# One kernel, five edits: the order of row sends, two accumulators for most experts, and the last sums on two engines

## The chip, the cores and the metric

The kernel runs on one core of a Trainium2 chip. The time is the device time of one execution in microseconds. Three runs of the kernel before gave 907.73, 908.15 and 908.41 us, median 908.15 us.

## The reference

The layer takes x of 8 batches, 512 rows, 256 features. The first half is attention in a window, the second half a mixture of 64 experts:

```
h = layernorm(x) * (1 + ca) + sa;   x = x + ga * attention(h)      # 16 heads, |q - k| <= 64
h = layernorm(x) * (1 + cb) + sb;   x = x + gb * experts(h)
# experts: sigmoid scores, 4 of 8 groups, 8 of 64 experts per row, weights * 2.5;
# at most 256 rows per expert; y = (silu(h Wg) * (h Wu)) Wd; every row adds up its 8 scaled y
```

All is float32 from outside; some products of the attention are in bf16 pieces.

## The kernel before, in words

There is no planner: every engine has its instruction stream written out in order, and semaphores tie the streams together. The work has two stages.

**Attention and routing.** Eight batches go through a loop (`body`) of 20 slots each: four groups of four heads (g), five key tiles (u), slot = 5g + u. A slot makes two tiles of scores, two exponentials on ScalarE (`exps`, L886, semaphore `exp`, two counts a slot), and VectorE takes maxima. The value products (`values`, L1159, semaphore `pv`, two counts a tile) are not made in their own slot: PE makes those of tiles 0, 1 and 2 of a group in slot u = 3, and those of tiles 3 and 4 in slot u = 0 of the next group (L1248 to L1250). Beside this, tables say in which slot the next batch is projected and the batch behind is normalised and routed. One step of these tables is `c_rstd` (L719): four small GpSimd operations that turn a half batch's variance (`mv2`, from VectorE, L1498) into the scale and shift that ScalarE then uses in `c_xhat` (L918). ScalarE works in order, so its exponentials stand behind `c_xhat`, and PE's scores wait for exponentials.

When a batch is routed, each of its rows goes to its 8 slots in DRAM (`slots_d`). That is 32 indirect DMAs a batch, issued by GpSimd (`send`, L731, and `send_some`, L751), up to two in a slot. The first of a slot waits until all exponentials of the slots before are done (count 2*slot). The second waits until all value products of the slots before are done (`pv`, count 2*slot, L757). GpSimd is in order too, so `c_rstd` of a later slot stands behind both. What is left of the last batches is sent after the loop: 8 sends of the last batch but one, `c_rstd(last, 0)`, 2 sends, `c_rstd(last, 1)`, 18 sends, and the 32 sends of the last batch (L807 to L820).

**Experts.** For each of the 64 experts SP loads 256 rows (`load_slots`, L634, a ring of 12), PE turns them, multiplies (L1394), and multiplies again (L1404); ScalarE scales the result into one of six buffers (`scale_y`, L1012), and GpSimd adds the rows into an accumulator in DRAM by two indirect DMAs (`scatter`, L822). There are three accumulators, `acc_d`. Expert e uses number `ACC[e]`, which is e % 3 up to expert 53 and e % 2 from there (L438). A scatter waits until the scatter before it into the same accumulator has landed (L842). Accumulator 0 starts as x. SP also loads weights, for experts 36 and up when the buffer of the expert 36 before is free (L650 to L652).

**The end.** SP loads accumulator 2 into `f2` (`load_f2`, L628, 32 DMAs of 128 KB) and the gates into `fg` (1 MB), waits for the last scatters, and loads accumulators 0 and 1 batch by batch into `fa` (L660, 16 DMAs of 512 KB). For each batch VectorE makes three operations of 128x1024 float32 (L1861, L1863, L1865): add the halves of `fa`, add `f2`, multiply by `fg`. SP stores each batch when its three are done (L665), in the order of the batches, all on the queue of the loads.

Of the kernel before, what the change touches and what calls it, by code (L numbers as in the profile page):

```python
# [25 lines left out]
ALU = mybir.AluOpType  # L26
# [19 lines left out]
HW = D + E + 4  # L46
# [18 lines left out]
    exp=10 * QUADS, pv=10 * QUADS, oTs=QUADS, oTp=QUADS, rec=QUADS, on=QUADS,  # L65
# [164 lines left out]
def build(nc, x, w_qkv, b_qkv, w_out, b_out, gate_w, gate_bias, w_gate, w_up, w_down, c, wmod, out):  # L230
    with ExitStack() as ctx:
        sems = {name: ctx.enter_context(nc.semaphore("s_" + name)) for name in PER}

        def sem(name):
            return ctx.enter_context(nc.semaphore(name))
# [20 lines left out]
        def after(eng, name, bt, k, apart=False):  # L256

            v = bt.b * PER[name] + k
            if isinstance(v, int) and v <= 0:
                return  # L260
            if apart or eng is nc.sync or eng is nc.gpsimd:
                hold(eng, sems[name], v)
            else:
                eng.wait_ge(sems[name], v)
# [31 lines left out]
        s_fg = sem("gate_rows_loaded")  # L296
# [18 lines left out]
        mod_d = dram("mod_d", [B, 5, D])  # L315
        slots_d = dram("slots_d", [SLOTROWS, HW])
        acc_d = [dram(f"acc_d{i}", [ACCROWS, D]) for i in range(3)]

        att = ExitStack()
        sb = lambda name, shape, dt=F32: sbt(att, name, shape, dt)  # L320
# [82 lines left out]
        sb = lambda name, shape, dt=F32: sbt(moe, name, shape, dt)  # L403
        NW, NX, NY = 36, 12, 6
# [3 lines left out]
        for i in range(NW):  # L408
# [8 lines left out]
        end = ExitStack()  # L417
        sb = lambda name, shape, dt=F32: sbt(end, name, shape, dt)
        fg = sb("fg", [P, B, D])
        sb("beyond_the_start", [P, 7656 - B * D])  # L420
        NF = 8
        f2 = [sb(f"f2_{i}", [P, T, D]) for i in range(B)]
        fa = [sb(f"fa{i}", [P, 2, T, D]) for i in range(NF)]
        end.close()
        eng_moe = dict(
            w_ld=[sem(f"weights_loaded{i}") for i in range(NW)],
# [3 lines left out]
            sg=sem("silu_done"),  # L430
            hm=sem("hidden_done"), yp=sem("expert_out_made"), yc=sem("expert_out_scaled"),
            f2_ld=sem("third_sums_loaded"),
            f_ld=[sem(f"sums_loaded{i}") for i in range(NF)], fsum=sem("last_sums"),
            f_st=sem("out_stored"),
        )
        mo = eng_moe

        ACC = [e % 3 if e < 54 else e % 2 for e in range(E)]  # L438
        NCONST = 26
        NSET = 4  # L440
        BLANKS = 32
# [33 lines left out]
        def rows_added(eng, e):  # L475

            eng.wait_ge(mo["y_st"][e % NY], 32 * (e // NY + 1))
# [21 lines left out]
        def _(sp):  # L499
# [125 lines left out]
            load_c(last)  # L625
            rows = slots_d.rearrange("(h p e) c -> p h e c", h=2, p=P)

            def load_f2(b):  # L628
                rows_added(sp, max(e for e in range(E) if ACC[e] == 2) + b)
                for t in range(T):  # L630
                    sp.dma_start(f2[b][:, t, :], acc_d[2][b * S:(b + 1) * S, :].rearrange("(p t) d -> p t d", p=P)[:, t, :]
                                 ).then_inc(mo["f2_ld"], 16)

            def load_slots(e):  # L634
                if e >= NX:
# [11 lines left out]
            for e in range(E):  # L647
                if NX <= e + 8 < E:
                    load_slots(e + 8)
                if e + NW < E:  # L650
                    sp.wait_ge(mo["yp"], e + 1)
                    load_w(slice(e + NW, e + NW + 1), e)  # L652

            for b in range(B):
                load_f2(b)
            sp.dma_start(fg[:], mod_d[:, 4, :].unsqueeze(0).to_broadcast([P, B, D])).then_inc(s_fg, 16)
            for e in range(E - NY, E):
                rows_added(sp, e)

            def load_f(i, n):  # L660
                for k in range(2):
                    sp.dma_start(fa[n][:, k], acc_d[k][0:N, :].rearrange("(b p t) d -> b p t d", b=B, p=P)[i]
                                 .rearrange("o p t d -> p (o t) d")).then_inc(mo["f_ld"][n], 16)

            def store_f(i, n):  # L665
                sp.dma_start(out[i].rearrange("o (p t) d -> p (o t) d", p=P), fa[n][:, 0]).then_inc(mo["f_st"], 16)

            for b in range(B):
                if b >= NF:
                    sp.wait_ge(mo["f_st"], 16 * (b - NF + 1))  # L670
                load_f(slice(b, b + 1), b % NF)
                if b >= NF - 1:
                    sp.wait_ge(mo["fsum"], 3 * (b - NF + 2))
                    store_f(slice(b - NF + 1, b - NF + 2), (b + 1) % NF)
            for b in range(B - NF + 1, B):
                sp.wait_ge(mo["fsum"], 3 * (b + 1))
                store_f(slice(b, b + 1), b % NF)
            sp.wait_ge(mo["f_st"], 16 * B)


# [1 line left out]
        def _(pool):  # L682
            gp = nc.gpsimd
            n = [0]
# [66 lines left out]
            def send_some(bt, rows, now, slot):  # L751

                for n, i in enumerate(rows):
                    if n == 0:
                        after(pool, "exp", now, 2 * slot)
                    else:
                        after(pool, "pv", now, 2 * slot)  # L757
                    send(bt, i)

            def body(prev, now, nxt):  # L760
# [61 lines left out]
            def scatter(e):  # L822
                begins = ACC[e] > 0 and ACC.index(ACC[e]) == e
                for h in range(2):
                    pool.wait_ge(mo["yc"], 2 * e + h + 1)
                    if begins:
                        pool.indirect_dma_start(
                            out=acc_d[ACC[e]][:, :], in_=ys[e % NY][:, h, :], in_offset=None,
                            out_offset=bass.IndirectOffsetOnAxis(ap=xg[e % NX][:, h, IDCOL:IDCOL + 1].bitcast(U32), axis=0),
                            bounds_check=last_acc, oob_is_err=True).then_inc(mo["y_st"][e % NY], 16)  # L830
                        continue
                    pool.indirect_dma_start(  # L832
                        out=acc_d[ACC[e]][:, :], in_=ys[e % NY][:, h, :], in_offset=None,
                        out_offset=bass.IndirectOffsetOnAxis(ap=xg[e % NX][:, h, IDCOL:IDCOL + 1].bitcast(U32), axis=0),
                        bounds_check=last_acc, oob_is_err=True, compute_op=ALU.add).then_inc(mo["y_st"][e % NY], 16)
# [3 lines left out]
            for e in range(E):  # L839
                same = [f for f in range(e) if ACC[f] == ACC[e]]  # L840
                if same:
                    rows_added(pool, same[-1])  # L842
                scatter(e)


        @block.scalar
        def _(act):
# [174 lines left out]
            for e in range(E):  # L1022
                silu(e)
                if e < E - 1:
                    take_x(e + 1)
                if e > 0:
                    scale_y(e - 1)
            scale_y(E - 1)

# [390 lines left out]
        def _(dve):  # L1420
# [434 lines left out]

            dve.wait_ge(s_fg, 16)
            dve.wait_ge(mo["f2_ld"], 16 * B * T)
            for b in range(B):
                a = fa[b % NF]
                dve.wait_ge(mo["f_ld"][b % NF], 32 * (b // NF + 1))  # L1860
                v.tensor_tensor(a[:, 0], a[:, 0], a[:, 1], ALU.add).then_inc(mo["fsum"], 1)  # L1861
                dve.wait_ge(mo["fsum"], 3 * b + 1)
                v.tensor_tensor(a[:, 0], a[:, 0], f2[b][:], ALU.add).then_inc(mo["fsum"], 1)  # L1863
                dve.wait_ge(mo["fsum"], 3 * b + 2)
                v.tensor_tensor(a[:, 0], a[:, 0], fg[:, b, :].unsqueeze(1).to_broadcast([P, T, D]), ALU.mult  # L1865
                                ).then_inc(mo["fsum"], 1)


_INS = ["L0_attn_x", "L0_attn_w_qkv", "L0_attn_b_qkv", "L0_attn_w_out", "L0_attn_b_out", "L0_ffn_gate_w",
# [18 lines left out]
```

## Time and profile before

| what | us |
|---|---|
| median of three runs | 908.15 |
| the profiled execution | 907.57 |
| its span, first to last instruction | 905.8 |
| PE busy | 681.8 (75%) |
| VectorE busy | 478.9 (53%) |
| ScalarE busy | 394.4 (44%) |
| GpSimd busy | 509.8 (56%) |

The span is what the rows below are measured in, from 0 to 905.8; 1.8 us of the profiled execution lie around it. An engine can be far from fully busy over the span and still set the end in one stage, so the stages are read one by one: attention from about 20 to 525, the rest of the routing to 613, experts from 613 to 868, the last sums from 868 to the end.

### The profile page before, as it was taken

The numbers are of one execution on the slowest core, as the hardware profiler recorded it, in microseconds if no ns is written. First come the engines' busy times: TensorE is split into PE (matmuls) and PEld (weight loads), VectorE is DVE, ScalarE is ACT, GpSimd is POOL, SyncE is SP. The second block draws the span as 40 slices with busy tenths as digits, with TensorE's granted clock in tenths as the row PEclk, the third lists the DMA queues.
The fourth block names the chain that finished last, engine by engine and source line by source line (L and its number), as shares of the span: only waits on it lengthen the run. The fifth ranks groups of instructions, "written<-read, shape, count | busy, mean of one in ns | idle before, by whom it ended". The sixth has DMA issues, their size and how long they took to land.

```text
span 905.8 us, 15461 instructions
## 1 busy us (share of the span) xinstructions
PE 681.8 (75%) x4760; PEld 466.9 (52%) x4787; DVE 478.9 (53%) x1964; ACT 394.4 (44%) x876; POOL 509.8 (56%) x519
## 2 busy tenths in 40 slices
PE   5679899999999999999797942006999888888000
PEld 3335556556566565565455522005888777676000
DVE  3065559869698697786787736201222222222048
ACT  2336566657566566665644511002444333334000
POOL 4000002057577476575767767772788888888810
PEclk9869999999999999999989975557999999999555
DMA  8684896748757577373536794107999998898997
GB/s 325 164 339 164 276 354 211 245 139 271 266 172 259 175 257 254 117 237 123 191 120 182 210 292 120 28 4 224 274 288 266 266 175 160 162 159 160 204 307 318
DMA packets 168334, 191.47 MB, mean 211 GB/s; under 512 B 22137, under 2 KB 150677, under 8 KB 168252
## 3 DMA queue, kind: packets, MB, share of 16 engines
q1 hardware_dynamic: 132220, 134.15, 46.6%
q0 software_dynamic: 30336, 38.03, 20.1%
q10 hardware_dynamic: 5696, 18.30, 5.3%
q8 instruction: 39, 0.64, 0.3%
q14 instruction: 43, 0.35, 0.1%
HBM read 100.64 MB, written 110.67 MB: 233 GB/s over the span
## 4 chain that ended last, share of the span: by engine, by line
PE 47%; POOL 14%; DMA 11%; DVE 10%; issue 9%; ACT 6%; ACTq 1%; SPq 1%; POOLq 0%; DVEq 0%
POOL acc_d L832 8%; PE outT L1171 7%; DMA acc_d<-ys,xg 7%; POOL slots_d L746 5%; PE scoresT L1394 5%; PE scoresT L1151 4%; PE stageA L1092 4%; PE scores L1129 4%; PE scoresT L1155 4%; PE stageA L1110 3%; PE stageC L1212 3%; ACT PT L890 2%; DMA Qs<-MT 2%; DVE junk L1453 2%; PE turns L1181 2%
## 5 line engine op out<-in xcount | busy, mean ns | idle before, releaser
L746 POOL DMA_INDIRECT slots_d<-H,dest x256 | 260.8, 1019 | 155.2 <-issue 87.9
L832 POOL DMA_INDIRECT acc_d<-ys,xg x124 | 191.6, 1545 | 55.0 <-issue 29.2
L1453 DVE CUSTOM_DVE_ANT_0 junk<-scores,mask 128x256 bf16<-128x256 f32 (+1 forms) x512 | 170.9, 387 | 72.1 <-PE scores L1129 70.8
L890 ACT ACTIVATE PT<-scoresT 128x512 f32<-128x512 f32 (+1 forms) x320 | 150.5, 509 | 47.5 <-PE scoresT L1155 45.6
L1394 PE MATMUL scoresT<-xgT,wgu 128*128 128x256 f32 x512 | 125.5, 388 | 17.5 <-ACT xgT L1005 17.4
L1151 PE MATMUL scoresT<-mask,identb 128*128 128x512 bf16 (+1 forms) x320 | 110.3, 345 | 18.7 <-ACT PT L890 14.5
L1394 PEld LDWEIGHTS scoresT<-xgT,wgu 128*128 128x128 f32 x512 | 95.4, 192 | 40.8 <-ACT xgT L1005 27.9
L1155 PE MATMUL scoresT<-Qs,Ks 98*128 98x256 bf16 (+1 forms) x640 | 110.9, 255 | 0.0
L1129 PE MATMUL scores<-Ks,Qs 96*128 96x256 bf16 (+1 forms) x512 | 93.7, 266 | 4.0 <-DVE mrowmax L1453 1.8
L1155 PEld LDWEIGHTS scoresT<-Qs,Ks 98*128 98x128 bf16 x640 | 64.0, 100 | 38.2 <-issue 8.6
L1171 PE MATMUL outT<-PT,Va 128*32 128x256 f32 (+1 forms) x1280 | 80.4, 356 | 1.8
L1842 DVE COPY xgT<-stageA 128x256 f32<-128x256 f32 x32 | 13.6, 425 | 118.2 <-PE stageA L1382 118.2
L874 ACT ACTIVATE parts<-stageA,bqk 128x512 bf16<-128x512 f32 x78 | 53.6, 687 | 42.3 <-PE stageA L1092 37.3
L1382 PE MATMUL scores<-ident,xg 128*128 128x128 f32 x128 | 24.9, 277 | 47.2 <-DMA xg<-slots_d 47.2
L1842 DVE COPY xgT<-stageC 128x256 f32<-128x256 f32 x32 | 13.6, 425 | 75.6 <-PE stageC L1382 75.6
L1151 PEld LDWEIGHTS scoresT<-mask,identb 128*128 128x128 bf16 x320 | 31.8, 99 | 39.8 <-ACT PT L890 22.2
L1005 ACT ACTIVATE xgT<-scores 128x256 f32<-128x256 f32 x64 | 24.7, 386 | 62.5 <-PE scores L1382 62.5
L1129 PEld LDWEIGHTS scores<-Ks,Qs 96*128 96x128 bf16 x512 | 44.4, 99 | 13.1 <-DVE mrowmax L1453 7.0
L1092 PE MATMUL stageA<-hT,wqkv 128*128 128x512 f32 x104 | 50.2, 605 | 0.0
L1171 PEld LDWEIGHTS outT<-PT,Va 128*32 128x32 f32 (+1 forms) x1280 | 28.9, 109 | 40.9 <-issue 25.2
L1018 ACT ACTIVATE ys<-outT,xg 128x256 f32<-128x256 f32 x64 | 26.9, 471 | 52.4 <-DMA acc_d<-ys,xg 45.3
L1018 ACT ACTIVATE ys<-turns,xg 128x256 f32<-128x256 f32 x64 | 26.9, 471 | 50.8 <-DMA acc_d<-ys,xg 43.1
(260 smaller groups left out, 1059.9 us busy)
## 6 DMA issues: line engine op xcount, KB each, us to landing
xg<-slots_d SPq DMA_DIRECT2D x64, 324.0 KB, 4.0
slots_d<-blank ACTq DMA_DIRECT2D x26, 648.0 KB, 5.2
parts_d<-parts SPq DMA_DIRECT2D x32, 384.0 KB, 3.4
Qs<-parts_d SPq DMA_DIRECT2D x96, 128.0 KB
Ks<-parts_d SPq DMA_DIRECT2D x90, 128.0 KB
acc_d<-zero SPq DMA_DIRECT2D x32, 272.0 KB
wgu<-L_ffn_w_gate_dram SPq DMA_DIRECT2D x64, 128.0 KB, 3.6
wgu<-L_ffn_w_up_dram SPq DMA_DIRECT2D x64, 128.0 KB, 3.7
```

What stands on the lines that cost most here:

```text
L746: pool.indirect_dma_start(out=slots_d[:, :], in_=H2[bt.par][:, t, :], in_offset=None, out_offset=bass.IndirectOffsetOnAxis(ap=dest[bt.par] ...
L832: pool.indirect_dma_start(out=acc_d[ACC[e]][:, :], in_=ys[e % NY][:, h, :], in_offset=None, out_offset=bass.IndirectOffsetOnAxis(ap=xg[e % ...
L874: sc_.activation(parts[:, j, k, :], bank[:, :], ACT.Identity, scale=SCALE if f < 2 else 1.0, bias=bqk[:, f:f + 1]).then_inc(sems["part"], 1)
L890: sc_.activation(PT[m % NPT][:, :, 0:w], src, ACT.Exp).then_inc(sems["exp"], 1)
L1018: sc_.activation(ys[e % NY][:, h, :], yb[:, h * D:(h + 1) * D], ACT.Copy, scale=xg[e % NX][:, h, D + e:D + e + 1]).then_inc(mo["yc"], 1)
L1092: last = mm(bank[:, :], wqkv[:, k, f * P:(f + 1) * P], hT[:, k, BAND:BAND + S], start=(k == 0), stop=(k == C - 1))
L1129: last = mm(bS[n % 2][:, i * 2 * P + lo:i * 2 * P + hi], q[0:MROW, h, t * P:(t + 1) * P], kk[0:MROW, h, t * P + lo:t * P + hi], start=True ...
L1151: mm(bST[m % 2][:, 0:2 * (hi - lo)].rearrange("p (h q) -> p h q", h=2), identb[:], half.unsqueeze(1).to_broadcast([P, 2, hi - lo]), start= ...
L1155: last = mm(bST[m % 2][:, i * (hi - lo):(i + 1) * (hi - lo)], kk[0:KROWS, h, u * P:(u + 1) * P], q[0:KROWS, h, lo:hi], start=False, stop=T ...
L1171: last = mm(bO[32 * j:32 * j + 32, lo:hi], Va[bt.par][rows, tile_of(u), HQ * g + j, :], PT[m % NPT][rows, i, 0:hi - lo], start=(u == 0), s ...
L1394: last = mm(bST[par][:, a * CAP:(a + 1) * CAP], wgu[e % NW][:, a, k, :], xgT[par][:, k, :], start=(k == 0), stop=(k == C - 1))
L1453: ins = v.tensor_tensor_reduce(out=junk[:, i, lo:hi], in0=bS[n % 2][:, i * 2 * P + lo:i * 2 * P + hi], in1=mask[:, lo:hi], scale=1.0, scal ...
```

## The change

- **Sends.** The second send of a slot waits for count 2*slot + 1 of `exp`, the slot's first exponential, and no longer for value products.
- **Accumulators.** `ACC[e]` is e % 3 up to expert 26 and e % 2 from there.
- **Third sums.** The 32 loads of `f2` are issued in the loop over experts, one in each of the iterations 27 to 58, each behind the expert's products, and the load of `fg` in iteration 59. They stood behind the loop. Four of the eight `f2` buffers lie in memory below the experts' own, the others behind it.
- **Last sums.** Batches 1 and 4 are summed by GpSimd, by the same three operations; VectorE sums the other six. The stores stay in the order of the batches, and all 16 loads of `fa` are issued ahead of the first store.
- **First output.** ScalarE scales the output of expert 0 in iteration 0, ahead of `silu(1)`; it stood in iteration 1.

```diff
-        ACC = [e % 3 if e < 54 else e % 2 for e in range(E)]
+        THIRD_ENDS = 27
+        POOL_SUMS = (1, 4)
+        ACC = [e % 3 if e < THIRD_ENDS else e % 2 for e in range(E)]
...
-            def load_f2(b):
-                rows_added(sp, max(e for e in range(E) if ACC[e] == 2) + b)
-                for t in range(T):
-                    sp.dma_start(f2[b][:, t, :], acc_d[2][b * S:(b + 1) * S, :].rearrange("(p t) d -> p t d", p=P)[:, t, :]
-                                 ).then_inc(mo["f2_ld"], 16)
+            def load_f2(b, t):
+                rows_added(sp, max(e for e in range(E) if ACC[e] == 2))
+                sp.dma_start(f2[b][:, t, :], acc_d[2][b * S:(b + 1) * S, :].rearrange("(p t) d -> p t d", p=P)[:, t, :]
+                             ).then_inc(mo["f2_ld"], 16)
...
-            for b in range(B):
-                load_f2(b)
-            sp.dma_start(fg[:], mod_d[:, 4, :].unsqueeze(0).to_broadcast([P, B, D])).then_inc(s_fg, 16)
+                if THIRD_ENDS <= e < THIRD_ENDS + B * T:
+                    sp.wait_ge(mo["yp"], e + 1)
+                    load_f2(*divmod(e - THIRD_ENDS, T))
+                if e == THIRD_ENDS + B * T:
+                    sp.wait_ge(mo["yp"], e + 1)
+                    sp.dma_start(fg[:], mod_d[:, 4, :].unsqueeze(0).to_broadcast([P, B, D])).then_inc(s_fg, 16)
...
-                    if n == 0:
-                        after(pool, "exp", now, 2 * slot)
-                    else:
-                        after(pool, "pv", now, 2 * slot)
+                    after(pool, "exp", now, 2 * slot + min(n, 1))
...
+            for n, b in enumerate(POOL_SUMS):
+                pool.wait_ge(mo["f_ld"][b], 32)
+                a = fa[b]
+                gp.tensor_tensor(a[:, 0], a[:, 0], a[:, 1], ALU.add).then_inc(mo["psum"], 1)
+                pool.wait_ge(mo["psum"], 3 * n + 1)
+                gp.tensor_tensor(a[:, 0], a[:, 0], f2[b][:], ALU.add).then_inc(mo["psum"], 1)
+                pool.wait_ge(mo["psum"], 3 * n + 2)
+                gp.tensor_tensor(a[:, 0], a[:, 0], fg[:, b, :].unsqueeze(1).to_broadcast([P, T, D]), ALU.mult
+                                 ).then_inc(mo["psum"], 1)
...
-                if e > 0:
+                if e == 0:
+                    scale_y(0)
+                if e > 1:
                     scale_y(e - 1)
```

## Rows read from the trace of the kernel before

**Rows 1.** The page's chain that ended last, shares by line.

```profile
POOL acc_d L832 8%; PE outT L1171 7%; DMA acc_d<-ys,xg 7%; POOL slots_d L746 5%; PE scoresT L1394 5%; PE scoresT L1151 4%; PE stageA L1092 4%; PE scores L1129 4%; PE scoresT L1155 4%; PE stageA L1110 3%; PE stageC L1212 3%; ACT PT L890 2%; DMA Qs<-MT 2%; DVE junk L1453 2%; PE turns L1181 2%
```

**Rows 2.** Windows: stretch, its us; busy of PE, PEld, DVE, ACT, POOL; clock; DMA; GB/s.

```profile
197.00:256.00 59.00, 55.61 (x467) 35.52 (x470) 47.35 (x221) 37.37 (x79) 38.78 (x46) 1.00 0.68 227
...
495.00:500.00 5.00, 4.21 (x30) 2.13 (x32) 3.36 (x11) 3.03 (x7) 3.25 (x4) 0.57 0.48 139
```

**Rows 3.** Timeline, slots 4 to 6 of the last batch: start, duration, instruction, idle before.

```profile
487.75 0.30 DVE L1498 BATCH_NORM_AGGREGATE mv<-stats 128x2 f32<-128x6 f32 x2
490.73 0.45 POOL L723 TENSOR_SCALAR ve<-mv 128x2 f32<-128x2 f32 x1
491.80 0.30 DVE L1498 BATCH_NORM_AGGREGATE mv<-stats 128x2 f32<-128x6 f32 x2
492.69 1.09 ACT L918 ACTIVATE H<-x,nmean,rs 128x256 f32<-128x256 f32 x2 [4.61 <-POOL nmean L729]
494.32 0.39 PE L1151 MATMUL scoresT<-mask,identb 128*128 128x512 bf16 x1 [3.03 <-ACT PT L890]
```

**Rows 4.** Timeline of GpSimd: first send of the last batch but one, and `c_rstd(last, 0)`.

```profile
525.70 0.97 POOL L746 DMA_INDIRECT slots_d<-H,dest  x1 [6.16 <-DVE H L1710]
...
541.13 0.22 POOL L723 TENSOR_SCALAR ve<-mv 128x2 f32<-128x2 f32 x1
```

**Rows 5.** Timeline of GpSimd: scatters of experts 3, 60, 62 and the last.

```profile
637.80 1.55 POOL L832 DMA_INDIRECT acc_d<-ys,xg  x1 [1.08 <-ACT ys L1018]
...
848.88 1.54 POOL L832 DMA_INDIRECT acc_d<-ys,xg  x1 [0.57 <-DMA acc_d<-ys,xg]
...
857.02 1.54 POOL L832 DMA_INDIRECT acc_d<-ys,xg  x1 [1.04 <-DMA acc_d<-ys,xg]
...
862.56 1.54 POOL L832 DMA_INDIRECT acc_d<-ys,xg  x1 [0.30 <-issue]
```

**Rows 6.** The last sums: timeline, the window 872 to 896, and the stores' issues.

```profile
868.36 8.87 SPq L662 DMA_DIRECT2D fa<-acc_d  x16
873.41 1.23 DVE L1861 TENSOR_TENSOR fa<-fa 128x1024 f32<-128x1024 f32 x1 [35.16 <-DMA fa<-acc_d]
901.50 1.22 DVE L1865 TENSOR_TENSOR fa<-fa,fg 128x1024 f32<-128x1024 f32 x1
872.00:896.00 24.00, 0.00 (x0) 0.00 (x0) 22.18 (x19) 0.00 (x0) 0.00 (x0) 0.50 1.02 410
L666 SPq DMA_DIRECT2D out_dram<-fa x8: 332/332/1058, 877.3 to 902.8; - x8
```

**Rows 7.** Scatters, issue to landing: stretch 690 to 726, then 726 to 827; timeline beside expert 58.

```profile
DMA to landing us min/median/max: 4.8/5.5/6.3
DMA to landing us min/median/max: 3.7/4.0/5.3
840.91 0.84 ACT L1018 ACTIVATE ys<-outT,xg 128x256 f32<-128x256 f32 x2 [3.11 <-DMA acc_d<-ys,xg]
```

**Rows 8.** Timeline: GpSimd and VectorE side by side, three places.

```profile
149.66 1.22 DVE L1514 TENSOR_TENSOR x<-x,mr 128x1024 f32<-128x1024 f32 x1
148.74 1.04 POOL L708 TENSOR_TENSOR rs<-ve,half_c 128x4 f32<-128x4 f32 x1
149.86 1.11 POOL L710 TENSOR_SCALAR nmean<-mv 128x4 f32<-128x4 f32 x1
142.99 0.24 POOL L727 TENSOR_SCALAR nmean<-mv 128x2 f32<-128x2 f32 x1
13.68 0.90 POOL L795 MEMSET Va<- 128x960 f32 x1
14.20 0.41 DVE L1439 COPY mcol<-modT 128x4 f32<-128x4 f32 x1
```

**Rows 9.** Timeline of GpSimd: a shorter memset and a copy.

```profile
12.80 0.55 POOL L791 MEMSET zero<- 128x544 f32 x1
111.00 0.29 POOL L717 COPY hT<-hT 128x128 f32<-128x128 f32 x1 [21.47 <-ACT hT L863]
```

More of the change, by code:

```diff
@@ L419, in build @@
         fg = sb("fg", [P, B, D])
-        sb("beyond_the_start", [P, 7656 - B * D])
+        f2 = [sb(f"f2_{i}", [P, T, D]) for i in range(B // 2)]
+        sb("beyond_the_start", [P, 7656 - B * D - B // 2 * T * D])
         NF = 8
-        f2 = [sb(f"f2_{i}", [P, T, D]) for i in range(B)]
         fa = [sb(f"fa{i}", [P, 2, T, D]) for i in range(NF)]
+        sb("beside_experts", [P, NW * 3 * D - NF * 2 * T * D + NX * 2 * HW + 2 * C * CAP + 4 * CAP + NY * 2 * D])
+        f2 += [sb(f"f2_{i}", [P, T, D]) for i in range(B // 2, B)]
         end.close()
@@ L432, in build @@
             f2_ld=sem("third_sums_loaded"),
-            f_ld=[sem(f"sums_loaded{i}") for i in range(NF)], fsum=sem("last_sums"),
+            f_ld=[sem(f"sums_loaded{i}") for i in range(NF)], fsum=sem("last_sums"), psum=sem("last_sums_by_gpsimd"),
             f_st=sem("out_stored"),
@@ L668, in _ @@
             for b in range(B):
[L669 to L677, printed above, removed]
+                load_f(slice(b, b + 1), b)
+            for b in range(B):
+                sp.wait_ge(mo["psum" if b in POOL_SUMS else "fsum"], 3 * sum((i in POOL_SUMS) == (b in POOL_SUMS) for i in range(b + 1)))
+                store_f(slice(b, b + 1), b)
             sp.wait_ge(mo["f_st"], 16 * B)
@@ L843, in _ @@
                 scatter(e)
+            pool.wait_ge(s_fg, 16)
+            pool.wait_ge(mo["f2_ld"], 16 * B * T)
+            for n, b in enumerate(POOL_SUMS):
[7 more added lines that the diff above has]
+                                 ).then_inc(mo["psum"], 1)
         @block.scalar
@@ L1857, in _ @@
             dve.wait_ge(mo["f2_ld"], 16 * B * T)
+            n = 0
             for b in range(B):
-                a = fa[b % NF]
-                dve.wait_ge(mo["f_ld"][b % NF], 32 * (b // NF + 1))
+                if b in POOL_SUMS:
+                    continue
+                dve.wait_ge(mo["f_ld"][b], 32)
+                a = fa[b]
                 v.tensor_tensor(a[:, 0], a[:, 0], a[:, 1], ALU.add).then_inc(mo["fsum"], 1)
-                dve.wait_ge(mo["fsum"], 3 * b + 1)
+                dve.wait_ge(mo["fsum"], n + 1)
                 v.tensor_tensor(a[:, 0], a[:, 0], f2[b][:], ALU.add).then_inc(mo["fsum"], 1)
-                dve.wait_ge(mo["fsum"], 3 * b + 2)
+                dve.wait_ge(mo["fsum"], n + 2)
                 v.tensor_tensor(a[:, 0], a[:, 0], fg[:, b, :].unsqueeze(1).to_broadcast([P, T, D]), ALU.mult
                                 ).then_inc(mo["fsum"], 1)
+                n += 3
 _INS = ["L0_attn_x", "L0_attn_w_qkv", "L0_attn_b_qkv", "L0_attn_w_out", "L0_attn_b_out", "L0_ffn_gate_w",
```

## The prediction

> **What bounds the kernel now.** I read the chain of waits first. No line holds more than 8% of it, and GpSimd's scatters and sends and their DMAs are high in it [rows 1]. So each stage has its own limit, and I went stage by stage.
>
> In the attention the windows show PE busy 55.6 of 59 us with GpSimd at 38.8 [rows 2]: PE paces it. One place is different. In the last batch VectorE has the first half's statistics at 488.05, but GpSimd begins `c_rstd` only at 490.73. ScalarE stands idle 4.61 us for it with its exponentials behind, and PE loses 3.03 us [rows 3]. The granted clock then reads 0.57 in 495 to 500 [rows 2], the lower level for most of that stretch. After the attention GpSimd sends without a pause: from 525.70, released by VectorE's routing, 12 sends stand ahead of `c_rstd(last, 0)` at 541.13 [rows 4]. What is gained before 525 therefore carries through to the experts.
>
> In the experts GpSimd is the bound. From expert 3 (637.80) to the last (862.56) are 121 steps between scatters. At 1.848 us each that is 223.6 of the 224.8 us between, and the two excesses of [rows 5] over the usual 0.30 idle (0.27 at 848.88, 0.74 at 857.02) are 1.0 of the rest. PE needs 3.03 us an expert (its products of the timeline stand so far apart from 627 to 694), GpSimd 3.70.
>
> In the last sums, `fa` loads are issued from 868.36 and the first batch is there at 873.4. VectorE's 24 operations run to 902.72, nearly back to back, 3.66 us a batch; the last store is issued at 902.8 and the shortest store takes 2.6 us. The DMA engines move 410 GB/s from 872 to 896 [rows 6]. VectorE is the bound, the DMAs close behind.
>
> **Sends.** The exponential of a slot is done long before the value products of the slots ahead. I put the send table, the ends of the 320 exponentials and the value products into a queue of 1.28 us per send. With the old wait it gives 490.67 for the late `c_rstd` (the trace: 490.73), with the new one GpSimd is free at 486.3. So it starts at 488.1, when the statistics are there, 2.6 us earlier. The next thing is then late: the second half's statistics end at 492.1 [rows 3], its `c_rstd` takes 1.65 us, and the next exponentials stand behind that half on ScalarE, from 494.9 and not 495.6. I take -0.6 us. Bounds: 0 if VectorE's four products behind it bind, and -3.7 if the 3 us stall and with it the lower clock go (2.5 to 3 us of PE's work between 496 and 502 ran at about half speed). In the other batches the queue shows `c_rstd` released by VectorE with either wait, so nothing there; no instruction is added.
>
> **First output.** ScalarE's scaling of expert 0 moves about 2.2 us forward into idle time. GpSimd waits for expert 3 (idle 1.08 at 637.80 [rows 5]), which this does not move. Cost and gain are 0; below and above by at most that 0.78 of excess.
>
> **Accumulators and third sums.** With two accumulators a scatter waits for the expert two before it. Its second scatter starts 3 x 1.85 = 5.55 us ahead, less 0.3 us of dispatch: no bubble if it lands within 5.25 us. The 840.91 row is expert 56 landing, 5.23 us after its start at 835.68; expert 58 then started on time. From 726 to 827 the landings by the profile's own count are 3.7 to 5.3 us, median 4.0; with weights loading beside them, 690 to 726, median 5.5 [rows 7]. ScalarE's waits (scale of e waits for e - 6) give the full delay of the slower scatter of experts 27 to 57: mean 4.7, four of 31 over 5.24, excess 0.3 us in sum. The `f2` loads put 128 KB beside each expert, a third of the weights' 384 KB. With landings 0.1 us later the excess is about 0.7 us: +0.7. Bounds: +0.3 with no delay, and +5.8 if they cost a third of the weights' 1.5 us (34 experts x 0.17).
>
> On SP the first `f2` load waits until expert 26 has landed (729.9), and `load_slots(36)` stands behind it. PE wants those rows at about 733.6 and gets them at 734.3; ScalarE then waits anyway until 737.0. Nothing is lost, and with that cover gone it is 1.7 us.
>
> In return the burst at the end goes. Both present bubbles lie under `f2` and `fg` loads: -1.0. The last scatter was issued at 862.56 and `fa` loads could start 5.8 us later; without a 1 MB load beside it I take the mean of 4.7 above and 0.2 for SP's start: -0.9.
>
> **Last sums.** VectorE loses 6 of 24 operations: 6 x 1.22 = 7.3 us. GpSimd gets six operations of 128x1024 with two inputs, of which the trace has none. A memset (no input) costs 0.90 for 960 and 0.55 for 544 elements: 0.84 ns an element and 0.10 fixed. The copy of 128 elements, 0.29 us, is 1.48 ns an element, so one input adds 0.65 [rows 8, 9]. Two inputs: 2.13 ns x 1024 + 0.10 = 2.3 us. Ends: 0.96 (the memset alone) and 3.2 (the copy's whole 0.29 per 128, plus a pass). I take 2.3, the copy being nearest.
>
> Can they run beside VectorE? A GpSimd operation of four elements that needs about 0.24 us took 1.11 us under a 1.22 us VectorE operation of just this kind (128x1024, both inputs in SBUF) and ended 0.09 us behind it. In the other direction a VectorE copy of four columns begun during the 0.90 us memset ended with it [rows 8]. So one waits for the other. VectorE and GpSimd then share 18 x 1.22 + 6 x 2.3 = 35.8 us, where VectorE alone took 29.3. Loads arrive one batch per 1.05 MB / 0.41 = 2.6 us and are ahead of this. The end moves by 13.8 - 7.3 = +6.5 us; by the ends of the price -1.5 and +11.9.
>
> The Trainium skill, "SBUF — State Buffer", section "Who interferes with whom", says that a VectorE instruction with two SBUF inputs contends with a GpSimd one that reads SBUF, and that the first to issue holds the shared pair for its whole instruction. The first part agrees with the 1.11 us; "whole" does not quite: the GpSimd operation of 148.74 to 149.78 reached 0.12 us into the VectorE one, which still took 1.22 [rows 8]. By "whole" the sum stays +6.5, by a hold of the reading alone it falls by some 0.1 us an operation, to +5.9. The Trainium skill, "GPSIMD Engine Reference", section "3.1 Elementwise — side-by-side cycle accounting", gives 4497 ns for 2048 elements; half of that is 2.25 us, which would make the term +6.2; no row here shows such an operation.
>
> **Sum.** +6.5 - 1.0 - 0.9 + 0.7 - 0.6 = +4.7 us on the span, 905.8 to 910.5. The profiled execution was 907.57, 0.6 under the median, so on the median: 912.9 us.
>
> **Rivals.**
> 1. *The engines run side by side* (faster). Then VectorE is done with its six batches at about 896.2, held up by loads, and the DMAs bind: 12.6 MB in all, of which 1.05 are in at 873.4, and 11.5 / 0.41 = 28.1 us more, 901.5 against 902.8 + 2.6 = 905.4 now: -3.9. With the other -1.8 this is 902.4 us. For: GpSimd is idle there. Against: the 1.11 us. It decides when six GpSimd operations cost VectorE less than 7.3 us together.
> 2. *Serial but cheaper, or the clock kept.* At 1.6 us an operation the term is +2.3, and with up to 3 us more in the last batch's attention the total lies at -2 to +2.5: 908.7. For: sizes are extrapolated eightfold. Against: the copy's slope.
> 3. *GpSimd shut out until VectorE pauses.* It then finishes batch 4 last, at the same 909, and the stores of 4 to 7 go out after it: 2.1 MB / 0.41 = 5.1 us where one took 2.6. 915.4.
> 4. *Two accumulators stall the scatters.* +5.8 for +0.7: 918.0. For: 5.5 us medians under loads. Against: 4.0 without.
>
> **Chances.** Forecast 0.50 (own range 910.5 to 914.5), rival 1 0.20, rival 2 0.20, rivals 3 and 4 0.05 each. 0.2% is 1.8 us, about what a measurement here can tell from no change. Faster by more: rival 1 and 0.08 of rival 2, 0.28. Within: 0.10 from rival 2. Slower by more: the forecast, rivals 3 and 4 and the rest of rival 2, 0.62. The range must reach rival 1's centre below and the forecast's worst above: 901 to 916.
>
> **What would show it.** Six GpSimd operations of 128x1024 of about 2.3 us or more, VectorE's 18 lengthened or with gaps of 2 us between them, and its last one ending near 907.4 (right); VectorE still 1.22 us beside them (rival 1). Idle before L723 near 490 with VectorE as releaser, and PE's stall moved to about 495. Scatters with idle over 0.30 released by a DMA between experts 27 and 63, some 0.7 us in sum. No `f2` load after 845. Wrong would be a GpSimd operation overlapping full-speed VectorE ones, or an excess over 3 us in the scatters.

## The result, and the profile after

| what | before | after |
|---|---|---|
| median of 12 runs, us | 907.87 (904.51 to 909.94) | 914.76 (911.01 to 923.15) |
| the profiled execution | 907.57 | 913.71 |
| its span | 905.8 | 911.9 |
| PE busy | 681.8 | 682.2 |
| VectorE busy | 478.9 | 481.9 |
| GpSimd busy | 509.8 | 527.6 |

The change makes the kernel slower: ratio 1.0089, 95% interval 1.0065 to 1.0112. That is 8.1 us (5.9 to 10.2); the two medians lie 6.9 us apart. The forecast was 912.9 us in a range of 901 to 916. GpSimd's extra 17.8 us come of its six sums. VectorE lost six operations and is still 3.0 us busier, which is the first sign of what happened.

Cut at the instants on which the prediction rests, the two profiled executions compare like this:

| stretch | before | after | difference |
|---|---|---|---|
| start to expert 3's scatter | 637.80 | 635.58 | -2.2 |
| expert 3's scatter to the last one | 224.76 | 229.69 | +4.9 |
| last scatter to VectorE's first sum | 10.85 | 8.93 | -1.9 |
| VectorE's first to last sum | 29.31 | 34.60 | +5.3 |
| from there to the end | 3.1 | 3.1 | 0 |

The sum is +6.1, which is 911.9 less 905.8. The chain of waits on the profile's page of the kernel after, shares by line, shows the growth in the scatters more roughly: the scatters, at 8% in [rows 1], are at 10%.

```profile
POOL acc_d L829 10%; PE outT L1182 7%; POOL slots_d L746 5%; PE scoresT L1405 5%; PE stageA L1103 5%; PE scoresT L1162 4%; DMA acc_d<-ys,xg 4%; PE scores L1140 4%; PE scoresT L1166 4%; PE stageA L1121 3%; PE stageC L1223 3%; ACT PT L899 2%; DVE junk L1464 2%; DMA Qs<-MT 2%; PE turns L1192 2%
```

**Last sums.** VectorE's timeline after, from its first sum (start, duration, instruction, idle before). In [rows 6] each of the 24 took 1.22 or 1.23.

```profile
874.20 1.23 DVE L1875 TENSOR_TENSOR fa<-fa 128x1024 f32<-128x1024 f32 x1 [32.82 <-DMA fa<-acc_d]
...
880.22 1.22 DVE L1875 TENSOR_TENSOR fa<-fa 128x1024 f32<-128x1024 f32 x1 [2.27 <-DMA fa<-acc_d]
881.47 3.25 DVE L1877 TENSOR_TENSOR fa<-fa,f 128x1024 f32<-128x1024 f32 x1
884.75 3.25 DVE L1879 TENSOR_TENSOR fa<-fa,fg 128x1024 f32<-128x1024 f32 x1
...
897.76 1.21 DVE L1875 TENSOR_TENSOR fa<-fa 128x1024 f32<-128x1024 f32 x1
...
907.57 1.23 DVE L1879 TENSOR_TENSOR fa<-fa,fg 128x1024 f32<-128x1024 f32 x1
```

And GpSimd's timeline after, for the same stretch:

```profile
877.80 2.34 POOL L847 TENSOR_TENSOR fa<-fa 128x1024 f32<-128x1024 f32 x1 [10.98 <-DMA fa<-acc_d]
880.22 3.42 POOL L849 TENSOR_TENSOR fa<-fa,f 128x1024 f32<-128x1024 f32 x1
883.72 3.20 POOL L851 TENSOR_TENSOR fa<-fa,fg 128x1024 f32<-128x1024 f32 x1
```

Read the two lists side by side. GpSimd's first sum runs while VectorE waits for loads and takes 2.34 us. Its other five each take 3.20 to 3.42 us and lie beside a VectorE sum that is lengthened as well. Five VectorE sums of 3.25 to 3.36, from 881.47 to 897.76, are five pairs. When GpSimd is done, VectorE is back at 1.21 at once.

**Scatters.** GpSimd's timeline after at four places that answer to [rows 5]: experts 3, 27, 56 and the last.

```profile
635.58 1.55 POOL L829 DMA_INDIRECT acc_d<-ys,xg  x1 [1.26 <-ACT ys L1027]
...
725.20 1.55 POOL L829 DMA_INDIRECT acc_d<-ys,xg  x1 [0.86 <-DMA acc_d<-ys,xg]
...
837.44 1.55 POOL L829 DMA_INDIRECT acc_d<-ys,xg  x1 [1.71 <-DMA acc_d<-ys,xg]
...
865.27 1.55 POOL L829 DMA_INDIRECT acc_d<-ys,xg  x1 [0.30 <-issue]
```

GpSimd's waits from 620 to 870 (waited for: us in total, times, longest), with the least, median and most from issue to landing of a scatter in 728 to 827 (4.0 in the middle in [rows 7]):

```profile
POOL acc_d L829 <- DMA acc_d<-ys,xg: 8.9, 12, 1.7
DMA to landing us min/median/max: 3.1/4.4/6.8
```

The idle before a scatter over the usual 0.30, released by a DMA, is called a bubble below. After expert 3 they add up to 5.2 us in ten places, where before they were 1.0 in two.

SP's timeline after, for the first row of [rows 6]: the loads of `fa` begin 3.92 us behind the last scatter, where it was 5.80.

```profile
869.19 9.30 SPq L667 DMA_DIRECT2D fa<-acc_d  x16
```

**Sends.** GpSimd's timeline after, for [rows 3] and [rows 4]: `c_rstd` of the last batch's halves, and the first send of the last batch but one.

```profile
488.08 0.23 POOL L723 TENSOR_SCALAR ve<-mv 128x2 f32<-128x2 f32 x1
...
491.93 0.22 POOL L723 TENSOR_SCALAR ve<-mv 128x2 f32<-128x2 f32 x1 [2.23 <-DVE mv L1509]
...
523.59 0.97 POOL L746 DMA_INDIRECT slots_d<-H,dest  x1 [6.35 <-DVE H L1721]
```

The first `c_rstd` starts at 488.08 and not 490.73; the second now waits for VectorE and no longer for sends. The windows after (us; busy of PE, PEld, DVE, ACT, POOL; clock; DMA; GB/s), of which the first answers to the second of [rows 2]; and the last one to that of [rows 6]:

```profile
495.00:500.00 5.00, 4.71 (x39) 2.55 (x40) 2.86 (x11) 1.95 (x5) 3.99 (x4) 0.67 0.43 124
500.00:505.00 5.00, 4.79 (x51) 3.17 (x50) 4.26 (x18) 3.33 (x8) 3.77 (x5) 0.99 0.56 160
872.00:896.00 24.00, 0.00 (x0) 0.00 (x0) 19.32 (x9) 0.00 (x0) 17.89 (x6) 0.50 0.99 393
```

The windows of the kernel before for the second of these stretches:

```profile
500.00:505.00 5.00, 4.86 (x40) 2.86 (x36) 2.04 (x11) 2.02 (x5) 3.78 (x5) 0.74 0.54 159
```

The granted clock is back at its upper level (2.4 GHz) almost from 500 on, and not only within 500 to 505. What that is worth can be read from ScalarE's exponentials. The timeline of the kernel before, the first one behind the second half's `c_xhat` and the one three slots later, in which 8.1 us pass:

```profile
495.63 1.07 ACT L890 ACTIVATE PT<-scoresT 128x512 f32<-128x512 f32 x2
...
503.76 0.38 ACT L890 ACTIVATE PT<-scoresT 128x256 f32<-128x256 f32 x1 [0.19 <-PE scoresT L1155]
```

And of the kernel after, in which 7.0 us pass:

```profile
494.66 1.06 ACT L899 ACTIVATE PT<-scoresT 128x512 f32<-128x512 f32 x2
...
501.62 0.91 ACT L899 ACTIVATE PT<-scoresT 128x256 f32<-128x256 f32 x2 [0.29 <-PE scoresT L1166]
```

### The profile page after: what moved, and what is told of

Same layout as the page of the kernel before. It is cut to its first block, busy times and chain, and to the rows that moved or that the text cites. A ratio compares the mean times of both kernels' runs of the same rounds, so it can differ in the third digit from the quotient of the medians.

```text
span 911.9 us, 15494 instructions
## 1 busy us (share of the span) xinstructions
PE 682.2 (75%) x4760; PEld 468.1 (51%) x4787; DVE 481.9 (53%) x1958; ACT 395.7 (43%) x876; POOL 527.6 (58%) x525
## 4 chain that ended last, share of the span: by engine, by line
PE 46%; POOL 16%; DVE 11%; issue 11%; DMA 9%; ACT 5%; SPq 1%; ACTq 1%; POOLq 0%; DVEq 0%
POOL acc_d L829 10%; PE outT L1182 7%; POOL slots_d L746 5%; PE scoresT L1405 5%; PE stageA L1103 5%; PE scoresT L1162 4%; DMA acc_d<-ys,xg 4%; PE scores L1140 4%; PE scoresT L1166 4%; PE stageA L1121 3%; PE stageC L1223 3%; ACT PT L899 2%; DVE junk L1464 2%; DMA Qs<-MT 2%; PE turns L1192 2%
## 5 line engine op out<-in xcount | busy, mean ns | idle before, releaser
L1162 PEld LDWEIGHTS scoresT<-mask,identb 128*128 128x128 bf16 x320 | 31.7, 99 | 37.8 <-ACT PT L899 18.7
L1393 PEld LDWEIGHTS scores<-ident,xg 128*128 128x128 f32 x128 | 18.3, 144 | 54.4 <-DMA xg<-slots_d 47.9
```

Source lines behind the costliest of these rows:

```text
L1162: mm(bST[m % 2][:, 0:2 * (hi - lo)].rearrange("p (h q) -> p h q", h=2), identb[:], half.unsqueeze(1).to_broadcast([P, 2, hi - lo]), start= ...
L1393: last = nc.tensor.transpose(bank[:, h * P:(h + 1) * P], xg[e % NX][:, h, k * P:(k + 1) * P], ident[:])
```

## The experiments

Every kernel but three was executed 6 to 12 times, beside the kernel before on the same chip; `x7_memsets`, `x9_first_output` and `x10_one_batch` were executed once, so only their profiles are read. The ratio is an estimate with its 95% interval and needn't equal the quotient of the two medians. Apart from the last sums, which are steady, executions differ by some 2 us (the last batch's attention starts at 470.6 to 474.0 in these profiles), so the profiles are compared by stretch. `x2`, `x3`, `x5`, `x6` and `x10` have the `f2` buffers where the changed kernel has them.

| kernel | us, beside before | ratio, 95% | bubbles | last scatter to first `fa` load | VectorE's sums |
|---|---|---|---|---|---|
| before | | | 1.01 | 5.80 | 29.31 |
| after | 914.76, 907.87 | 1.0089 (1.0065 to 1.0112) | 5.23 | 3.92 | 34.60 |
| x1_sends | 905.77, 906.48 | 0.999 (0.9968 to 1.0013) | 1.50 | 6.45 | 29.31 |
| x2_two_accumulators | 909.93, 906.48 | 1.0045 (1.0026 to 1.0064) | 7.30 | 3.88 | 29.32 |
| x3_two_engines | 913.14, 906.48 | 1.009 (1.0066 to 1.0114) | 0.47 | 6.94 | 34.89 |
| x4_all_but_two_engines | 906.79, 906.48 | 1.0015 (0.9993 to 1.0037) | 4.74 | 3.86 | 29.32 |
| x5_two_accumulators_late_loads | 905.55, 907.07 | 0.9981 (0.9963 to 0.9999) | 2.73 | 6.56 | 29.32 |
| x6_three_accumulators_other_loads | 906.56, 907.07 | 0.9993 (0.9975 to 1.001) | 2.73 | 3.94 | 29.32 |
| x7_memsets | 904.56, 907.07 | | 6.55 | 3.81 | 23.83 |
| x8_sends_gates_early | 903.16, 907.07 | 0.9957 (0.9934 to 0.998) | 0.90 | 3.95 | 29.32 |
| x9_first_output | 908.49, 905.55 | | 1.62 | 6.62 | 29.32 |
| x10_one_batch | 908.08, 905.55 | | 0 | 6.14 | 31.85 |

### The two engines

`x3_two_engines` is the kernel before with the last sums of the change alone; `x4_all_but_two_engines` is the changed kernel without them.

```diff
# x3: before, with the change's loops of sums, loads and stores, and
-        ACC = [e % 3 if e < 54 else e % 2 for e in range(E)]
+        THIRD_ENDS = 54
+        POOL_SUMS = (1, 4)
+        ACC = [e % 3 if e < THIRD_ENDS else e % 2 for e in range(E)]
# x4: after
-        POOL_SUMS = (1, 4)
+        POOL_SUMS = ()
```

> The kernel before with batches 1 and 4 of the last sums on GpSimd and all loads of them ahead of the first store, and nothing else. My theory (the two engines hold each other up): VectorE's operations beside a GpSimd one take about 3.25 us and not 1.22, its last one ends about 34.6 us after its first instead of 29.3, +5.3 us (+4 to +6.5). Rival (the longer end came of loads that landed late because of the early loads): VectorE at 1.22 us throughout, -3.9 to 0 us.

> The changed kernel with all eight last sums on VectorE. My theory: the parts add up, sends -2.1, accumulators and early loads +3: +0.9 us against before (-0.5 to +2.5), and the last sums back at 29.3 us. Rival (the loads of the last sums land later because of the rest, so the last sums stay long): +4 us or more.

Measured: 1.009 for the first, 1.0015 for the second, whose interval holds 1. The edit alone costs what the whole change costs, and without it nothing is left that can be told from no change. VectorE's sums came out as expected (34.89 and 29.32 us). The time of `x3_two_engines` is 6.7 us above before by the medians, just over the 6.5 that was expected at most. VectorE's timeline in `x3_two_engines`, second batch:

```profile
880.90 3.41 DVE L1875 TENSOR_TENSOR fa<-fa 128x1024 f32<-128x1024 f32 x1 [2.39 <-DMA fa<-acc_d]
884.35 3.24 DVE L1877 TENSOR_TENSOR fa<-fa,f 128x1024 f32<-128x1024 f32 x1
```

GpSimd's second sum begins at 880.90 as well. It takes 2.34 us, and here it is VectorE's that is lengthened; after, both began at 880.22, and GpSimd's was. Why the turn falls out one way or the other isn't shown. The wait for the second batch (2.39 here, 2.27 after) is there again. Dropping batch 1 from VectorE's list lets it ask for batch 2 before that is loaded.

`x7_memsets` asks why the pairs are slow. GpSimd makes six memsets on the same buffers in place of its six sums. Each writes twice the elements of a sum, in 1.84 us, and reads nothing; batches 1 and 4 are left out of the output.

```diff
-                a = fa[b]
-                gp.tensor_tensor(a[:, 0], a[:, 0], a[:, 1], ALU.add).then_inc(mo["psum"], 1)
...
+                for k in range(3):
+                    if k:
+                        pool.wait_ge(mo["psum"], 3 * n + k)
+                    gp.memset(fa[b][:], 0.0).then_inc(mo["psum"], 1)
```

> The changed kernel with GpSimd's six sums replaced by six memsets of 128x2048 (about 1.8 us each by the memsets of 128x544 and 128x960): batches 1 and 4 are not summed. They write SBUF and read nothing there. Theory A (the two engines meet at the reading of two inputs): VectorE's operations stay at 1.22 us, the last sums take about 22 us of VectorE's time plus waits for loads, 24 to 26 us, and the span ends some 6 us sooner than the changed kernel's 911.9. Theory B (any GpSimd operation on SBUF keeps VectorE's two-input operations out): they take about 3 us beside a memset.

Measured: three memsets, 5.53 us in all, with VectorE's sums beside them at full speed. GpSimd's timeline of `x7_memsets`:

```profile
877.20 5.53 POOL L849 MEMSET fa<- 128x2048 f32 x3 [9.96 <-DMA fa<-acc_d]
884.83 5.53 POOL L849 MEMSET fa<- 128x2048 f32 x3 [2.10 <-DMA fa<-acc_d]
```

VectorE's timeline of `x7_memsets`, two of its sums in those stretches:

```profile
880.95 1.23 DVE L1874 TENSOR_TENSOR fa<-fa,f 128x1024 f32<-128x1024 f32 x1
...
885.86 1.22 DVE L1876 TENSOR_TENSOR fa<-fa,fg 128x1024 f32<-128x1024 f32 x1
```

VectorE's stretch is 23.83 us, of which 1.63 are waits for loads. The span ends at 902.7, 9.2 us ahead of the kernel after, though 4.3 us are left behind VectorE's last sum and not 3.1. So the transfers allow a shorter end, and a busy GpSimd is no obstacle: what holds VectorE up goes away when GpSimd no longer reads. The Trainium skill, "SBUF — State Buffer", section "Who interferes with whom", says just this: a VectorE instruction with two SBUF inputs contends with a GpSimd one that reads SBUF, and not with one that only writes it. The 1.22 us agree.

`x10_one_batch` checks the price by its count: one batch of GpSimd's in place of two, three pairs in place of five, and no batch that VectorE reaches too early.

```diff
# x3, with
-        POOL_SUMS = (1, 4)
+        POOL_SUMS = (4,)
```

> As the two-engine run, but GpSimd sums batch 4 alone. My theory (a VectorE operation beside a GpSimd one costs it 2.0 us more, 3.27 from start to start and not 1.25): three such pairs cost 6.1 us, three operations fewer save 3.7, so VectorE's last sums take 29.3 + 2.4 = 31.7 us (31.3 to 32.2). Rival (the cost is that of the whole GpSimd share being on the path, 3 x 2.34 = 7.0 for 3.7): 32.6 us or more. Rival (side by side): 25.7 us, or what the loads allow.

Measured: VectorE's stretch 31.85 us. GpSimd's timeline of `x10_one_batch`, and below it VectorE's:

```profile
885.88 3.20 POOL L851 TENSOR_TENSOR fa<-fa,f 128x1024 f32<-128x1024 f32 x1
```

```profile
882.38 1.22 DVE L1875 TENSOR_TENSOR fa<-fa 128x1024 f32<-128x1024 f32 x1
883.64 3.25 DVE L1877 TENSOR_TENSOR fa<-fa,f 128x1024 f32<-128x1024 f32 x1
```

From start to start a pair takes 3.28 us (in x3 884.35 to 887.63), where the two operations alone take 1.22 + 2.34 = 3.56. It costs VectorE 3.25 - 1.22 = 2.03 us. The Trainium skill, "SBUF — State Buffer", section "SBUF: two separate sides", says that of such a pair the one that starts first gets the shared ports for its whole instruction and the other is blocked. By that the pair would take the sum, an estimate of 3.56 us, and the runs show 0.28 less. Three pairs cost 6.1 and three operations dropped save 3.7: 29.3 + 2.4 = 31.7, against 31.85. The rival, by which all three of GpSimd's operations are on the path (32.6), is out. For two batches: five pairs 10.2, the wait 2.3, six operations saved 7.3, so +5.2, against +5.3 after.

### The accumulators and the loads of the third sums

`x2_two_accumulators` is the kernel before with these two edits of the change, and all sums on VectorE. `x5_two_accumulators_late_loads` has the two accumulators from expert 27 on, but the loads at the end as before. `x6_three_accumulators_other_loads` keeps three accumulators up to expert 53 and makes as many loads of the same size at experts 27 to 58, from the input x; the third sums are left out of its output.

```diff
# x2
-        ACC = [e % 3 if e < 54 else e % 2 for e in range(E)]
+        THIRD_ENDS = 27
+        ACC = [e % 3 if e < THIRD_ENDS else e % 2 for e in range(E)]
# ... and load_f2(b, t), fg in the loop over experts, as in the change
# x5: ACC as x2, the loads behind the loop
-                rows_added(sp, max(e for e in range(E) if ACC[e] == 2) + b)
+                rows_added(sp, 53 + b)
# x6: the loads as x2, ACC as before
-                sp.dma_start(f2[b][:, t, :], acc_d[2][b * S:(b + 1) * S, :]...
+                sp.dma_start(f2[b][:, t, :], x[b]...
```

> The kernel before with two accumulators from expert 27 and the early loads of the third sums and the gates, and nothing else. My theory: bubbles on GpSimd released by a landing scatter, 5 us in sum over experts 28 to 63 (+4.3 over before, which has 1.0), and the last sums begin about 1.9 us sooner behind the last scatter: +3 us (+1.5 to +4.5). Rival (two accumulators cost nothing and the bubbles were an accident of that execution): -1.5 to -3 us.

> The kernel before with two accumulators from expert 27, but the third sums and the gates loaded as before, in a burst from expert 53 on. My theory (two accumulators leave the scatters no slack, and the loads beside them take the rest): between experts 28 and 52 few bubbles, 0.5 to 1.5 us in sum, and more under the burst, 1 to 3 us; the gap from the last scatter to the first load of the last sums stays at about 5.8 us. Time +1 to +3 us. Rival A (the accumulators alone do it): 4 us or more of bubbles before expert 53. Rival B (the loads alone): none before expert 53.

> The kernel before with three accumulators up to expert 53, and the 32 loads of 128 KB at experts 27 to 58 and the load of the gates as in the changed kernel, but from x in place of the third accumulator: the third sums are left out of the output. My theory: with three accumulators a scatter may land up to 9.2 us after its issue, so the same loads cost no bubble before expert 56, and the gain at the last sums (-1.9 us) stays: -1.5 to -2.5 us. Rival (the loads hold the scatters up by themselves, as with two accumulators): 4 us of bubbles, +2 us or more.

Measured. The waits of GpSimd from 620 to 870 (total, times, longest) and the landings in 728 to 827, of `x2_two_accumulators`:

```profile
POOL acc_d L832 <- DMA acc_d<-ys,xg: 11.8, 15, 1.9
DMA to landing us min/median/max: 2.8/4.7/6.9
```

Of `x5_two_accumulators_late_loads`:

```profile
POOL acc_d L831 <- DMA acc_d<-ys,xg: 4.5, 6, 1.1
DMA to landing us min/median/max: 3.7/4.2/5.9
```

Of `x6_three_accumulators_other_loads`:

```profile
POOL acc_d L832 <- DMA acc_d<-ys,xg: 3.0, 1, 3.0
DMA to landing us min/median/max: 3.6/5.4/7.1
```

Set the second line against the first in each. Loads raise the median landing from 4.0 to 5.4 in `x6`, and three accumulators bear that: no bubble before expert 56. Two accumulators alone, in `x5`, have landings at 4.2 and 1.7 us of bubbles before expert 54. Both together have, before expert 54, 5.0 us in `x2`, 3.3 in `x4`, 3.9 in `x7` and 3.4 after; before has none. The allowance of 5.25 us explains it. In 728 to 827, 1 of 54 scatters landed later than that in the kernel before, 4 of 45 in `x5`, 16 of 52 after, 24 of 43 in `x2` and 31 of 54 in `x6`, whose third accumulator takes it up. So most of the stall comes of the longer landing against the shorter allowance; the shorter allowance alone makes a smaller part.

The one bubble of `x6` tells of another thing, the burst at the end. SP's timeline of `x6_three_accumulators_other_loads`:

```profile
824.96 1.88 SPq L634 DMA_DIRECT2D f<-L_attn_x_dram  x4
829.32 0.38 SPq L661 DMA_DIRECT2D fg<-mod_d  x1
```

And GpSimd's:

```profile
838.12 1.54 POOL L832 DMA_INDIRECT acc_d<-ys,xg  x1 [3.03 <-DMA acc_d<-ys,xg]
```

Four loads of 128 KB and the 1 MB of gates go out within 5 us. The kernel after has them too (823.26 and 828.19), and its longest bubble, at 837.44 in the fence of scatters above. So the burst was not taken away but moved forward, and the bubble there is 1.4 us, in `x6` 2.7; in both kernels the accumulators are two from expert 54 on. Which of the burst's loads makes it isn't shown.

In whole time `x2` is slower by 0.45% (0.26 to 0.64), 2.4 to 5.8 us, as expected; its profile has 6.3 us more of bubbles, 2 more than expected, and 1.9 less in the gap. `x6` can't be told from before (expected: 1.5 to 2.5 us faster): its one bubble took back what the gap gave. For `x5` the time was expected 1 to 3 us longer and came out at 0.9981 (0.9963 to 0.9999), 0.1 to 3.4 us shorter. That is a miss. Its profiled execution was its slowest, with a span of 909.8, and what the 1.7 us of bubbles in it are worth in the time isn't shown.

### Sends, gates and first output

`x1_sends` is the edit of the sends alone. `x8_sends_gates_early` adds one more to it: the 1 MB of gates, which depend on nothing in this stage, is loaded at expert 32 and not at the end.

```diff
# x1 and x8
-                    if n == 0:
-                        after(pool, "exp", now, 2 * slot)
-                    else:
-                        after(pool, "pv", now, 2 * slot)
+                    after(pool, "exp", now, 2 * slot + min(n, 1))
# x8 also
+                if e == 32:
+                    sp.dma_start(fg[:], mod_d[:, 4, :].unsqueeze(0).to_broadcast([P, B, D])).then_inc(s_fg, 16)
...
-            sp.dma_start(fg[:], mod_d[:, 4, :].unsqueeze(0).to_broadcast([P, B, D])).then_inc(s_fg, 16)
```

> The kernel before with the edit of the sends alone. My theory: the stall beside expert routing in the last batch shrinks, the first send of the last batch but one starts near 523.6 instead of 525.7, and all behind it comes 2.1 us earlier: time -2.1 us (-1.0 to -3.5), no change in the stretch from the first scatter to the end. Rival (the sends make no difference, and the 2 us seen in the changed kernel come from a granted clock that differs from run to run): within 0.5 us of before.

> A version meant to beat both: the kernel before with the edit of the sends, and the 1 MB load of the gates at expert 32 in place of the end. Theory: sends -2 us, and the last scatter lands without the load beside it, so that the last sums begin 1 to 2 us sooner: -3 us (-1.5 to -4.5) against before. Rival (the burst of the third sums alone keeps the landing late): -2 us only.

Measured. From the last batch's first exponential to the first send of the batch before it, the seven kernels without the edit have 53.1, 53.3, 53.4, 53.5, 53.9, 54.2 and 54.5 us; those with it 51.3 (after) and three times 51.2, and `x8` 53.3. So the edit brings some 2 us in four of five profiles. Whether the fifth differs by chance of one execution isn't shown. What differs in it can be seen in the windows of `x8_sends_gates_early`:

```profile
500.00:505.00 5.00, 4.80 (x41) 3.00 (x38) 1.36 (x9) 1.64 (x4) 3.78 (x5) 0.64 0.45 139
```

The granted clock is 0.64 in 500 to 505, low as before (0.74), where after has 0.99. `x8` is some 1.6 us behind after at this place, so the windows don't cut the same work. Over the 8 us from the same exponential the clock was 0.57 before and in `x8`, and 0.79 after and in `x1`. In time, `x1` is inconclusive: 0.999, and its interval holds both no change and 2 us; by the medians it gained 0.7 us, less than the 1.0 expected at least. So what the sends' edit gives in time isn't shown.

That gap is what the second edit of `x8` is about. GpSimd's last scatter in `x8_sends_gates_early`:

```profile
863.09 1.54 POOL L830 DMA_INDIRECT acc_d<-ys,xg  x1 [0.30 <-issue]
```

And SP's timeline of the same kernel:

```profile
867.04 9.01 SPq L663 DMA_DIRECT2D fa<-acc_d  x16
```

3.95 us lie between, with the `f2` loads still where they were. Of all kernels those with the gates at the end have 5.8 to 6.9, those with the gates earlier 3.8 to 4.0. `x8` runs at 0.9957 (0.9934 to 0.998) of the kernel before, 3.9 us less by the medians. 1.9 us of it are the gap. The rest could be the 2 us of the sends, but its own profile doesn't have them. It beats the kernel before, and the one after, which stands at 1.0089 of before.

`x9_first_output` is the last part alone.

```diff
-                if e > 0:
+                if e == 0:
+                    scale_y(0)
+                if e > 1:
```

> The kernel before with the output of expert 0 scaled in iteration 0, and nothing else. Theory: the first scatter comes 2.4 us sooner behind the last send (14.3 us instead of 16.7), expert 3's at the same 26.4 us, and the time is that of before. Rival (the two experts that begin accumulators let the stream start sooner): expert 3's scatter and the end 1 us or more sooner.

Measured, GpSimd's timeline of `x9_first_output`, its first scatter and expert 3's:

```profile
625.33 1.58 POOL L832 DMA_INDIRECT acc_d<-ys,xg  x1 [13.67 <-ACT ys L1018]
...
637.34 1.55 POOL L832 DMA_INDIRECT acc_d<-ys,xg  x1 [1.26 <-ACT ys L1018]
```

The last send was issued at 610.68. The first scatter stands 14.65 us behind it, where before it was 16.7; expert 3's stands 26.66 behind it, where it was 26.45. The gain of 2 us is waited off before expert 3. One execution, 908.49 us beside 905.55, says nothing finer of the time.

## Why the prediction was right, step by step

- **Last sums, +6.5 forecast, +5.3 measured.** The mechanism was right for this pair of operations: one engine waits for the other, a GpSimd operation takes 2.34 us (2.3 forecast), VectorE's last sum ends at 908.8 (902.7 before, 907.4 forecast). `x3` and `x4` show that the loss is this edit's; `x7` that it hangs on GpSimd's reading; `x10` that the price is 2.03 us a pair. One of the two rows behind it was no evidence. The VectorE copy that ended with a memset [rows 8] has one input, and the sums, which have two, run at 1.22 us beside a memset in `x7`: who waits depends on what both do, and that GpSimd can hold up a sum was a guess that came true. Two things stand against the forecast's +6.5, and they partly cancel. The two operations overlap by 0.28 us in each pair (the prediction had some 0.1 as a variant), and one of GpSimd's six ran alone. Against this, VectorE waits 2.3 us for batch 2: "loads arrive one batch per 2.6 us and are ahead of this" failed, since batch 2 was there at 880.2, 11 us after the first load was issued, and VectorE no longer had batch 1 to do. The forecast's own figures said so: at 2.6 us a batch, batch 2 is there 5.2 us after batch 0, and VectorE is done with batch 0 in 3.7. In the trace after, batch 2 was there 6.0 us after batch 0. Rivals 1 and 3 are refuted: the five VectorE sums took 3.25 to 3.36 us, and GpSimd was done at 896.75, long before VectorE.
- **Accumulators and third sums, +0.7 - 1.0 forecast.** The sum of the two was -0.3 and the runs show +4.9: the loss was foreseen in kind and mis-sized by far. The stretch from expert 3 to the last scatter went up by 4.9 us, and bubbles from 1.0 to 5.2. An excess over 3 us in the scatters was among the prediction's own signs of being wrong, and it came. The step that failed is "with landings 0.1 us later". In the median they came 0.4 us later after (4.4) and 1.4 us in `x6` (5.4); the largest went from 5.3 to 6.8, and it is the late ones that meet a limit of 5.25 us: 16 of 52, where there was 1 of 54. The upper bound, +5.8 from 0.17 us an expert, held, but how 0.17 follows from a third of 1.5 us isn't worked out there. The bubbles make 4.2 of the 4.9 us. The other 0.7 is 6 ns a step (1.855 for 1.849 us). `x3` and `x10` have 1.855 too, and the kernels without sums on GpSimd at the end, `x7` with memsets among them, have 1.848 or 1.849. So this part goes with the last edit, not with the accumulators; why, the runs don't show. The other failed step is "the burst at the end goes": part of it only moved, to 823 to 829, and the accumulators are two there as well. Rival 4's mechanism, at +5.8 and given 1 in 20, is what happened in this term; it was mistaken to have it as a whole case beside the forecast rather than as a term inside it.
- **Last scatter to the loads, -0.9 forecast, -1.9 measured.** The direction was right. The 1 MB of gates, not the `f2` loads, held the last landings, as `x8` shows. The term that was mis-sized is the landing without them: 4.7 us was the mean of the slower scatter of experts 27 to 57, and the whole gap became 3.92.
- **Sends, -0.6 forecast, -2.1 in the profile.** The steps came as they were put: `c_rstd` 2.65 us earlier, right behind its statistics, and the exponentials at 494.66 (494.9 forecast). 0.3 us of the 2.1 was there already when the last batch began (472.56 and 472.24), so up to those exponentials the edit brought 0.65 us. What the term left out is the clock, which stood only in its bound (-3.7) and in rival 2. From those exponentials three slots took 7.0 us in the profiles after and of `x1`, `x4` and `x7`, 1.2 us less than before. Of the kernels without the edit they took 7.5 us in `x10`, 7.9 in `x9`, 8.1 in before, `x3`, `x5` and `x6`, and 8.3 in `x2`; with it, in `x8`, 8.1. PE's idle stretch ahead was 1.7 us where they took 7.0 (1.75 after), 1.95 in `x8`, and 3.0 to 4.1 in the others.
- **First output, 0 forecast.** Right, by the mechanism named.

The terms of the forecast were +4.7 together and the profile shows +6.1. The scatters came out 5.2 us above their two terms (+4.9 for -0.3), the other terms together 3.8 below theirs: the total was near by luck, because the errors have opposite signs. By the medians the change is +6.9 us. The parts alone give +6.7 (`x3`), +3.5 (`x2`) and -0.7 (`x1`), 9.5 together; part of why the whole is less may be that `x3` keeps the long gap before the `fa` loads (6.94), which the whole has not (3.92). The intervals, each of some 2 us either way, can hold the rest.

## What to carry to other kernels

Before work is given to a second engine, look whether the two can read memory at once; where the trace shows one waiting for the other in operations of the same kind, count each pair as almost the sum of both. Where a chain of transfers has a fixed allowance (here 5.25 us), count the landings that exceed it under the traffic that the change adds; a median doesn't show them. A large load in flight beside the last short transfers is paid for by them: with the 1 MB of gates moved ahead, and the sends' edit, the kernel is faster than either version.

## What the runs showed of the hardware

- Elementwise operations with two inputs, 128x1024 float32, alone 1.22 us on VectorE and 2.34 on GpSimd, take 3.25 and 3.20 side by side, a new pair every 3.28 us. A GpSimd memset of 128x2048, 1.84 us, slows VectorE's not at all (1.22 or 1.23 us in `x7`). The Trainium skill, "GPSIMD Engine Reference", section "3.1 Elementwise — side-by-side cycle accounting", gives 4497 ns for 2048 elements; by halving that is an estimate of 2.25 us for 1024, and the trace has 2.34.
- The scatter with addition into DRAM lands in 4.0 us in the median beside the loads of rows alone (before), 5.4 beside one more load of 128 KB per expert (`x6`). From the last scatter it takes 5.8 to 6.9 us to SP's next load with the 1 MB of gates loaded at the end, and 3.8 to 4.0 with it loaded earlier.
- After a shorter stall, PE's next three slots took 7.0 us and not 8.1, at a granted clock of 0.79 and not 0.57 over 8 us. Why `x8` with the same edit took 8.1 and `x10` without it 7.5 stays open, as does what makes a pair 0.28 us shorter than its parts.
- The step from scatter to scatter is 1.855 us in the three kernels in which GpSimd makes sums at the end, and 1.848 or 1.849 in the nine others. The cause is open.
